# Attention with a routed low-rank layer: first steps of the attention loop in another order on VectorE and GpSimd

## The reference, cut to what matters

```python
q = rope((layernorm(x) @ wq).reshape(...))         # 32 heads of 128
k = rope((ctx @ wk).reshape(...))                  # 8 heads, each for 4 query heads
v = (ctx @ wv).reshape(...)
attn = softmax(q k^T / sqrt(128) + mask)
x = x + tanh(g_xattn) * (attn @ v) @ wo
h = layernorm(x)
logits = h @ route_w.T                             # best of 8 experts
x = x + tanh(g_ffn) * (top logit of the best expert) * ((h @ A_best.T) @ Bw_best.T)
```

## Time and profile before

| what | value |
|---|---|
| median of 3 runs | 1104.44 us (1104.04 to 1106.16) |
| the profiled execution | 1103.77 us, of which span 1101.4 |
| PE busy | 1088.9 us, 99% of the span |
| PE weight load busy | 918.4 us, 83% |
| DVE busy | 882.0 us, 80% |
| ACT busy | 642.3 us, 58% |
| POOL busy | 593.1 us, 54% |
| mean granted clock of PE | 0.998 |
| the chain that ended last | PE 85%, issue 4%, DVE 4%, POOL 3% |

### The profile page before, as it was taken

The page is one execution under the profiler, slowest core; times in us unless marked ns, Lnnn a source line. Parts: engine busy times, 40 slices in busy tenths (PEclk is TensorE's granted clock), DMA queues, the critical chain, the costliest instruction groups (busy, mean ns, idle before and its releaser), DMA issues.

```text
span 1101.4 us, 16992 instructions
## 1 busy us (share of the span) xinstructions
PE 1088.9 (99%) x5628; PEld 918.4 (83%) x5628; DVE 882.0 (80%) x1410; ACT 642.3 (58%) x1111; POOL 593.1 (54%) x518
## 2 busy tenths in 40 slices
PE   9999999999999999999999999999999999999998
PEld 7888888778888888888888888888888888888886
DVE  7876757888888888888887998777777777777887
ACT  7563466675666666666656544555555555555543
POOL 5552488787777777777754333333333333333423
PEclk9999999999999999999999999999999999999999
DMA  7859973595546464646389546453535353533202
GB/s 258 265 209 350 375 251 142 178 382 167 202 162 210 154 210 155 210 154 210 136 305 375 178 135 222 141 194 114 187 114 185 114 185 107 182 106 115 67 11 77
DMA packets 106085, 206.26 MB, mean 187 GB/s; under 512 B 8848, under 2 KB 58640, under 8 KB 100112
## 3 DMA queue, kind: packets, MB, share of 16 engines
q1 hardware_dynamic: 105712, 204.79, 54.9%
q10 hardware_dynamic: 288, 0.39, 0.1%
HBM read 122.31 MB, written 82.84 MB: 186 GB/s over the span
## 4 chain that ended last, share of the span: by engine, by line
PE 85%; issue 4%; DVE 4%; POOL 3%; SPq 2%; DMA 1%; ACT 1%; DVEq 0%; POOLq 0%; ACTq 0%
PE attn L924 30%; PE proj L858 28%; PE score L875 10%; PE attn L820 4%; PE attn L909 3%; PE attn L911 3%; PE turned L886 2%; PE score L820 2%; PE turned L820 2%; DMA v_kept<-vst 1%; SPq L560 1%; PE small L975 1%; SPq L584 1%; POOL rstd L1730 1%; POOL rot L1784 0%
## 5 line engine op out<-in xcount | busy, mean ns | idle before, releaser
L924 PE MATMUL attn<-wo_s,o_s 128*128 128x512 f32 x1524 | 374.8, 395 | 0.0
L858 PE MATMUL proj<-xB,wq_s 128*128 128x512 f32 x1344 | 335.0, 392 | 0.0
L924 PEld LDWEIGHTS attn<-wo_s,o_s 128*128 128x128 f32 x1524 | 280.8, 188 | 56.9 <-DVE o_s L1234 0.2
L858 PEld LDWEIGHTS proj<-xB,wq_s 128*128 128x128 f32 x1344 | 252.8, 189 | 53.1 <-issue 1.9
L1784 POOL TENSOR_TENSOR rot<-rot,tab 128x512 f32<-128x512 f32 x110 | 161.3, 1466 | 149.2 <-ACT rot L1527 149.0
L1572 ACT ACTIVATE o_s<-attn 128x512 fp32r<-128x512 f32 x127 | 69.4, 595 | 120.0 <-PE attn L911 120.0
L875 PEld LDWEIGHTS score<-k_r,q_r 128*128 128x128 f32 x1024 | 123.9, 191 | 7.9 <-issue 1.9
L1141 DVE TENSOR_TENSOR q_r<-q_r,tab 128x512 f32<-128x512 f32 x128 | 123.9, 968 | 1.5 <-ACT x_third L1527 1.4
L875 PE MATMUL score<-k_r,q_r 128*128 128x64 f32 x1024 | 121.3, 271 | 0.8 <-DVE prob_even L1207 0.8
L1226 DVE TENSOR_TENSOR p_low<-turned,p_high 64x512 fp32r<-64x512 f32 x128 | 87.9, 687 | 17.1 <-ACT p_high L1564 14.8
L1548 ACT ACTIVATE copies<-proj 128x512 f32<-128x512 f32 x96 | 57.5, 599 | 74.3 <-PE proj L858 74.1
(11 more groups left out here) (250 smaller groups left out, 1649.3 us busy)
## 6 DMA issues: line engine op xcount, KB each, us to landing
wq_kept<-wq_s SPq DMA_DIRECT2D x16, 1792.0 KB, 6.3
wq_s<-wq_kept SPq DMA_DIRECT2D x16, 1792.0 KB, 8.4
v_kept<-vst SPq DMA_DIRECT2D x64, 256.0 KB, 4.3
v_s<-v_kept SPq DMA_DIRECT2D x128, 128.0 KB, 4.9
wo_kept<-wo_s SPq DMA_DIRECT2D x32, 512.0 KB, 4.9
wo_s<-wo_kept SPq DMA_DIRECT2D x32, 512.0 KB, 5.4
k_kept<-kst SPq DMA_DIRECT2D x32, 256.0 KB, 2.4
wq_raw<-in_wq SPq DMA_DIRECT2D x16, 512.0 KB, 8.4
```

The costliest lines, as they stand in the source:

```text
L858: last = e.matmul(dst[:, :], wq_s[:, b % 2, A, s, kt, :], xB[:, B, mv, kt, :], start=(first and kt == 0 and m == 0), stop=(kt == 1 and m = ...
L924: last = e.matmul(out_bank(k, bp)[:, :], o_s[:, s, bp, h, :], wo_s[n % WO_SLOTS][:, m, :], start=(h == 0 and i == 0), stop=(h == GROUP - 1 ...
```

## The change

Three things are put in another order; no instruction is added or taken away.

1. Zeros and last key. POOL sets the zeros of `p_low` before the sine of the last key's rope, not behind it. DVE makes the low halves of step 0 before it adds that rope. `times_values(0)` no longer waits for both last keys at its start: each of its two banks waits for the rope of its own key.
2. POOL in step 2. The first two sums of weights (`combine_weights(4, (0,))`) come before `normalise(2)`, and the low half of wo 4 goes from behind `normalise(2)` to the end of the step. The wait for rope (2, 3) ahead of `weight_low(4, 0)` is left out in this step.
3. DVE's ropes. Rope (2, 2) moves from before the low halves of step 2 to behind the second `add_out` of that step. Rope (2, 3), whose cosine and add stood on the two sides of the first low half, moves into step 3, behind `q_sum`. ACT, which shifts, and POOL, which multiplies by the sine, keep their order of the ropes.

```diff
--- before.py
+++ after.py
@@ -892,17 +892,18 @@
                 tiles = [s * PAIRS + bp for bp in range(PAIRS)]
                 e.wait_ge(v_in[u % 2], 80 * (u // 2 + 1))
                 e.wait_ge(probs_low, 2 * k + 2)
-                if k == 0:
-                    e.wait_ge(*drained["attn"])
                 cols = [slice(bp * GROUP * SEQ, (bp + 1) * GROUP * SEQ) for bp in range(PAIRS)]
                 for bp in range(PAIRS):
-                    if k + 1 == STEPS:
+                    if k == 0:
+                        e.wait_ge(rope_added, ROPE_NO[JOBS[bp - PAIRS]] + 1)
+                    elif k + 1 == STEPS:
 
                         if bp == 0:
                             e.wait_ge(masked, STEPS)
                         else:
                             e.wait_ge(x1_added, 2 * k - 1)
-                    elif k:
+                    else:
                         e.wait_ge(x1_added, 2 * k - 1 + bp)
                     b = out_bank(k, bp)
                     for twin in range(2):
@@ -1003,7 +1004,6 @@
                     scores(0)
 
             drained[turned.name] = rope_added, ROPE_NO[JOBS[-3]] + 1
-            drained["attn"] = rope_added, ROPE_NO[JOBS[-1]] + 1
 
             first, middle, last = products_of(0)
             for b, i in first + middle:
@@ -1349,8 +1349,8 @@
 
             for q in sums_of(0)[0]:
                 q_sum(*q)
+            prob_low(0, 0, 1)
             finish_key(len(JOBS) - 1)
-            prob_low(0, 0, 1)
             for k in range(1, WIDE):
                 early, late = sums_of(k)
                 ropes = ropes_of(k)
@@ -1371,26 +1371,26 @@
                 for q in sums_of(k - 1)[1] + early:
                     q_sum(*q)
 
-                for q in (ropes_of(0)[0], ropes_of(1)[0])[k - 1] if k <= 2 else ():
+                for q in ropes_of(k - 1)[0] if k <= 3 else ():
                     q_cos(*q)
                     q_add(*q)
-                if k > 1:
+                if k > 2:
                     ropes_left(k - 1)
                 between(k, 2)
                 add_out(k - 1, 0)
                 between(k, 3)
-                for q in ropes[0] if k > 1 else ():
+                for q in ropes[0] if k > 2 else ():
                     q_cos(*q)
                 between(k, 4)
                 if k % 4 != 3:
                     prob_low(k, 0)
-                for q in ropes[0] if k > 1 else ():
+                for q in ropes[0] if k > 2 else ():
                     q_add(*q)
                 prob_low(k, *((0, 1) if k % 4 == 3 else (1,)))
                 between(k, 5)
                 add_out(k - 1, 1)
-                if k == 1:
-                    ropes_left(0)
+                if k <= 2:
+                    ropes_left(k - 1)
                 between(k, 6)
                 between(k, 7)
                 between(k, 8)
@@ -1807,6 +1807,10 @@
                     x_norms(X_BESIDE[n])
                 if n == SCORES_AFTER:
                     subtract_max(0)
+                if n == ZEROS_BESIDE:
+                    e.wait_ge(rope_added, FOUR.stop)
+                    e.memset(p_low[:, :, :, :].bitcast(F32), 0.0).then_inc(zeros_set, 1)
                 if JOBS[n][0] == "k":
                     by_sin(ROPE_NO[JOBS[n]])
                 if n == SCORES_AFTER:
@@ -1821,9 +1825,6 @@
                     weight_low(*w)
                 for w in SPLITS_BESIDE.get(n, ()) if not early else ():
                     raw_low(w)
-                if n == ZEROS_BESIDE:
-                    e.wait_ge(rope_added, FOUR.stop)
-                    e.memset(p_low[:, :, :, :].bitcast(F32), 0.0).then_inc(zeros_set, 1)
             combine_weights(HEAD_PAIRS + 1, (0,))
             for k in range(1, WIDE):
                 ropes = ropes_of(k)
@@ -1833,16 +1834,13 @@
                     for q in ropes_of(0)[0]:
                         by_sin(ROPE_NO["q", *q])
                 elif k % 2 == 0 and pieces:
-                    if k > 2:
-                        combine_weights(pieces[0][0], (0,))
+                    combine_weights(pieces[0][0], (0,))
                 elif k % 4 == 1:
                     for n in wo_late(k - 1):
                         raw_low(("wo", n))
                 elif pieces:
                     weight_low(*pieces[0])
                 normalise(k)
-                for n in wo_late(1) if k == 2 else ():
-                    raw_low(("wo", n))
                 if k == 1:
                     for w in weights_of(0):
                         weight_low(*w)
@@ -1850,21 +1848,21 @@
                         by_sin(ROPE_NO["q", *q])
                     combine_weights(HEAD_PAIRS + 1, (1,))
                 if k % 2 == 0 and pieces:
-
-                    combine_weights(pieces[0][0], (1,) if k > 2 else (0, 1))
+                    combine_weights(pieces[0][0], (1,))
                 for q in ropes[0]:
                     by_sin(ROPE_NO["q", *q])
                 if k % 2 and pieces:
                     weight_low(*pieces[0 if k % 4 == 1 else 1])
                 if k % 2 == 0 and pieces:
-
-                    e.wait_ge(rope_added, ROPE_NO["q", *ropes[0][0]] + 1)
+                    if k > 2:
+                        e.wait_ge(rope_added, ROPE_NO["q", *ropes[0][0]] + 1)
                     weight_low(*pieces[0])
                 for q in ropes[1] + ropes[2]:
                     by_sin(ROPE_NO["q", *q])
                 if k % 4 != 3 and pieces:
                     weight_low(*pieces[1])
-                for n in wo_late(k) if k % 4 and k > 1 else ():
+                for n in wo_late(1) if k == 2 else wo_late(k) if k % 4 and k > 1 else ():
                     raw_low(("wo", n))
                 for t in norms_of(k):
                     inverse_std(("expert", t))
```

## The result

| | before | after |
|---|---|---|
| median | 1103.98 us (17 runs, 1102.91 to 1106.16) | 1106.66 us (17 runs, 1104.49 to 1109.06) |
| profiled execution | 1103.77, span 1101.4 | 1104.49, span 1102.7 |

The ratio is 1.0022, with a 95% interval of 1.0016 to 1.0028: slower by 2.4 us (2.7 between the medians). The time lies in the predicted range (1102.0 to 1107.3), 1.3 us above the predicted 1105.4 and just above the forecast's own range, which ended at 1106.6. The direction was given as +1.0; the loss is more than twice that. It is just over the 0.2% (2.2 us) that the prediction named as about what can be told from no change.

A forecast was written before the change was run, and what follows sets the result against it. PE, busy 99%, was taken as the bound, with 5.47 us at most to win from two stops and the clock. -0.65 at scores(4) plus 1.63 of clock gave +1.0 on 1104.44: 1105.4 us, range 1102.0 to 1107.3.

The forecast's parts named there:

- the forecast's own range: Run time of the main forecast, 1104.2 to 1106.6 us, given chance 0.50.
- The main path: PE's three gaps become one long stop before scores(4), with low clock behind it: +1.0 us, chance 0.50.
- First edit: Stop before times_values(0) falls to about 0.3 us; of 0.8 us gained, 0.45 is lost waiting for normalise(2), 0.35 kept.
- Second edit: POOL's two sums, 0.74 us each, fit its 1.70 us wait, normalise(2) isn't late; later fetch of wq_raw is hidden.
- The stop before times_values(2): The 2.69 us stop goes, and its 1.63 us of clock; PE comes at 245.6.
- The new stop: Before scores(4), released by VectorE's rope add: four ropes take 9.6 us, PE stops 4.0 us, scores(4) starts at 260.8.
- The clock: Falls once behind the stop at scores(4), charged 1.63 us as behind the old 2.69 us stop.
- (a): Lighter contention: four ropes in 7.6 us, 2.0 us stop at scores(4), clock holds: -2.7 us, 1101.8; chance 0.17.
- (b): Change simply works: ropes within 5.7 us, no stop at scores(4): -4.7 us, 1099.8; chance 0.05.
- (c): Slower VectorE: four ropes 11.3 us, scores(4) at 262.5, +2.7 us with the clock, 1107.1; chance 0.16.
- (d): Clock holds through the 4.0 us stop at scores(4): -0.65 us, 1103.8; chance 0.12.
- Long ropes beside GpSimd: VectorE's ropes contend with GpSimd for SBUF and stay long wherever put beside POOL's queue: cosine 1.74 us against 0.68.

The follow-up runs named there:

- (2): Kernel before with only the reorder of zeros and last key: 1104.3 us, ratio 1.0005.
- (3): Kernel before with only the reorder of POOL's sums and low half in step 2, wait for rope (2, 3) kept: 1102.19 us, ratio 0.9985.
- (1): The changed kernel measured again, with no edit: 1106.88 us, ratio 1.0027 to the kernel before.
- (8): Changed kernel with GpSimd's low half of wo 5 put off from step 3 into step 4: 1109.6 us, ratio 1.0043 to before.
- (5): Changed kernel with ropes (2, 1) and (2, 2) put ahead of sum_rows(2): 1110.25 us, ratio 1.0046 to before.
- (4): Kernel before with only DVE's ropes moved, and POOL's wait ahead of weight_low(4, 0) gone: 1106.99 us, ratio 1.0029.
- (6): Changed kernel, ropes (2, 1), (2, 2) ahead of sum_rows(2), rope (2, 3) behind step 2's second add_out: 1103.88 us, ratio 0.9994 to before.
- (9): Kernel before with the zeros/last-key and POOL step 2 reorders, without the moved ropes: 1102.91 us, ratio 0.9988.

## Why the prediction was right or wrong

The main path was right: the old stops go, one new stop comes before scores(4), released by VectorE's rope, and the clock falls behind it. The term of the sum that was mis-sized is the clock. The account of the first edit was wrong beyond its first stop, and some of the agreement in absolute times is luck.

- **First edit: right at its stop, wrong behind it.** The stop at times_values(0) was to be about 0.3 and is 0.28. Of the 0.8 us gained 0.45 was to be given back at turn_probs(2) and 0.35 kept. All of it is given back: counted from scores(1), turn_probs(2) is 25.22 us on, for 25.11 before. The prediction let the exponent follow a VectorE that is 0.2 earlier; it left out that ScalarE's shift waits for the last key's add, now 1.54 us, so that exponent and normalising come 0.1 later. Alone, (2), the edit is worth nothing.
- **Second edit: right as to cost, too modest as to worth.** It costs nothing, as predicted: the sums are 0.74 us each, 0.30 of idle time is left, and SP's wq_raw goes out at 249.46, where 249 was expected, with no wait on it. That it wins 1.7 us alone (3) wasn't seen: it brings the sine forward for which VectorE idled 1.25 us in before.
- **The stop before times_values(2): right.** It is gone, and the clock is full there. That PE was to come at 245.6 and comes at 245.59 is luck: the trace runs 0.26 us ahead, and the 0.35 us of the first edit never arrived.
- **The new stop: right in place and releaser, and its end within 0.3 us.** scores(4) was predicted for 260.8 and starts at 260.84, which on the time scale of before is 261.1, 0.3 late; in (1) it is 261.1 too (261.48, with a start 0.39 later). The four ropes are 10.3 us for 9.6; the rest of the queue is 0.5 us shorter, most of it from the mask to the reciprocal of step 3, 4.15 us for 4.47. The stop is 3.45 for 4.0, since PE itself is ready later, 0.27 us of it by turn_probs(3). So the gain up to scores(4) is 0.20 and not 0.65. For 0.3 VectorE is late, which the earlier start of the trace hides. For 0.16 I had set the chain's start of scores(4) (261.46) against the new start, while the timeline has 261.30: the chain begins a piece where the one before it ends.
- **The clock: the term that was mis-sized.** I charged 1.63 us once, since the stop was "longer than the 2.69 us after which the clock fell". It fell, but the low stretch is 3.4 us long in one execution (1.73 us lost) and 6.8 in another (3.34), and 12 of 17 executions have the mean clock of the second. With -0.2 and 3.3 the sum is +3.1, with 1.7 it is +1.5; and the median of after, +2.7, lies among the runs of the dearer kind. The price had been read from one execution of before, of the cheaper kind. By the traces 1.6 us of what is missing in the predicted +1.0 is this. The time itself came closer than the loss (1.3 us off for 1.7), because the three runs of before that it was added to had a median 0.46 above that of all 17; that too is luck.
- **The rivals.** (a) asked for four ropes in 7.6 us: they took 10.3. It also let the clock hold after 2.0 us, and in (3) it fell after 1.35. (b) fell with it. (c) forecast nearly the measured time, but by ropes of over 10.9 us, which they weren't: its time is right for another reason. (d), a clock that holds, was shown wrong by both traces.
- **Long ropes beside GpSimd: right, but not for each part.** (8) takes GpSimd's work away from one such add and it falls from 1.56 to 0.69 us; in (5) four parts beside GpSimd are all above 1.0. But in after the add at 253.34 takes 0.69 although a product of GpSimd starts at 253.42, and there it is GpSimd's that is long, 1.77 us. The Trainium skill (GPSIMD Engine Reference, Key points) has the two contend where VectorE's instruction has two inputs in SBUF. The traces agree; that such ropes stay long wherever GpSimd is busy, as the prediction drew from it, goes too far.

Open: what decides between a low stretch of 3.4 and of 6.8 us. The 6.8 was seen once behind a stop of 2.69 (2) and once behind 3.43 (1), the 3.4 behind 2.69 (before), 3.45 (after), 3.43 (4), 3.10 (6), 1.35 (3), and both stops of (5) and of (8). That it is more frequent behind the new stop than behind the old is read from the mean clocks of the runs; why, no run here tells.

## What to carry to other kernels

An in-order engine that is nearly full pays for a late rope somewhere: before work is put off, sum its queue up to the next point where PE waits for it, with the long durations wherever GpSimd has products of its own beside it. Put work into the engine's own idle time instead, and no more than about fits there: in before's order of ropes one early won, in the changed order two lost. Moving an instruction back also delays those on other engines that wait for it, as the last key's add did on ScalarE. Of several edits that were made together, run each alone: here one was worth 1.7 us, one nothing, and one lost 3.1. Price a stop with the clock behind it from several executions, not from one, and align two traces at an instruction ahead of the change before their times are subtracted.

## What the runs showed of the hardware

- In the attention loop the clock fell after a stop of PE of 1.35 us in one execution (3) and held after 1.36 in another (9). It fell after each of the ten stops from 2.56 to 3.45 us in these traces, and in no trace after one of 1.16 us or less.
- Its low stretches were 3.4 or 6.8 us long, behind stops of one length. A stretch of 3.4 cost 1.6 to 1.7 us (before, after, (4)). One of 6.8 cost 3.3 us where all of it lay behind the stop (1), and 2.7 where its first 1.0 us lay in the stop (2).
- A product or a sum of VectorE with both inputs in SBUF (128x512) takes 0.67 to 0.69 us alone and mostly 1.0 to 1.8 beside GpSimd; where VectorE's began first it took 0.69 and GpSimd's stretched (1.77 for 1.27, after at 253.34 and (6) at 256.54). VectorE's `add_out`, with an input in PSUM, stays at 0.73 to 0.75 in the same stretches.
